# A gated cross-attention and local-attention block on one core: residual held transposed, rotary products on POOL, one ring of two PSUM banks, loops unrolled

## What is computed

```python
def attn_layer(x, Wqkv, qs, ksc, Wo):            # HEADS = 16, DIM_HEAD = 64, INNER = 1024
    q, k, v = jnp.split(x @ Wqkv, 3, -1)
    q = l2norm(q) * qs                           # per head
    k = l2norm(k) * ksc
    q = q * cos * scale + rotate_half(q) * sin * scale
    k = k * cos * inv + rotate_half(k) * sin * inv
    out = local_attention(q, k, v)               # windows of 32, each sees itself and the one before
    return out @ Wo
def ffn_layer(x, g, bln, W1, b1, W2, b2):        # inner width 341
    a, gate = jnp.split((layernorm(x) * g + bln) @ W1 + b1, 2, -1)
    return a * gelu(gate) @ W2 + b2
for i in range(6):
    x = attn_layer(shift_tokens(x), ...) + x     # shift_tokens: channels 64 to 127 come from the token before
    x = ffn_layer(shift_tokens(x), ...) + x
```

## Time and profile before

| | us |
|---|---|
| median of 3 runs | 2334.8 (2331.06 to 2336.24) |
| profiled execution, span from first to last instruction | 2340.2 |
| PE busy | 1958.2 |
| DVE busy | 1954.2 |
| ACT busy | 1449.0 |
| POOL busy | 1158.9 |

### The profile page before, as it was taken

How to read it: one execution, slowest core, us unless ns; L and a number is a source line. 1 busy time by engine, 2 the same in 40 slices (tenths; PEclk the granted TensorE clock), 3 DMA queues, 4 the chain that set the end, 5 groups by cost and what they waited for, 6 DMA issues and landing times.

```text
span 2340.2 us, 62168 instructions
## 1 busy us (share of the span) xinstructions
PE 1958.2 (84%) x19682; PEld 1270.3 (54%) x19682; DVE 1954.2 (84%) x3398; ACT 1449.0 (62%) x2645; POOL 1158.9 (50%) x868
## 2 busy tenths in 40 slices
PE   6678888888888888888888888888888888888886
PEld 4455555555555555555555555555555555555554
DVE  4689888888898898888888988888889889888784
ACT  2366666676666666666756666666666666666563
...
DMA packets 164546, 130.64 MB, mean 56 GB/s; under 512 B 42123, under 2 KB 157881, under 8 KB 164281
## 3 DMA queue, kind: packets, MB, share of 16 engines
...
...
## 4 chain that ended last, share of the span: by engine, by line
DVE 50%; issue 24%; PE 11%; ACT 9%; DVEq 3%; POOL 2%; ACTq 0%; DMA 0%; SPq 0%; POOLq 0%
DVE ra L1063 13%; DVE ss L1100 8%; DVE qkn L998 5%; DVE o L1096 5%; DVE rs L1069 4%; DVE mx L1004 4%; PE bank L716 3%; POOL rb L1188 2%; ACT qk L770 1%; ACT seed L788 1%; ACT L899 1%; DVE ssm L1103 1%; PE bank L527 1%; DVE step L987 1%; DVE step L984 1%
## 5 line engine op out<-in xcount | busy, mean ns | idle before, releaser
L1203 POOL TENSOR_TENSOR qkn<-qkn,rn 128x512 f32<-128x512 f32 x192 | 239.6, 1248 | 812.8 <-DVE rn L990 812.8
L1188 POOL TENSOR_TENSOR rb<-qk,tables 128x512 f32<-128x512 f32 x384 | 572.7, 1501 | 139.2 <-ACT qk L770 139.2
L527 PE MATMUL bank<-wqkv,xsT 128*128 (+1 forms) x1152 | 581.2, 614 | 12.6 <-ACT qk L770 10.3
L1063 DVE TENSOR_TENSOR ra<-qk,tables 128x512 f32<-128x512 f32 x384 | 467.1, 1255 | 92.1 <-issue 75.0
L1196 POOL TENSOR_TENSOR qkn<-ra,rb 128x512 f32<-128x512 f32 x192 | 268.6, 1399 | 122.6 <-DVE ra L1063 105.6
L770 ACT ACTIVATE qk<-bank 128x512 f32<-128x512 f32 x384 | 226.9, 591 | 158.2 <-PE bank L527 158.2
L527 PEld LDWEIGHTS bank<-wqkv,xsT 128*128 128x128 f32 x1152 | 192.9, 192 | 143.4 <-issue 118.7
L779 ACT ACTIVATE pr<-pr 128x512 f32<-128x512 f32 x192 | 120.9, 630 | 203.0 <-DVE pr L1007 198.6
L851 ACT ACTIVATE kB<-bank 64x512 f32<-64x512 f32 x384 | 226.4, 590 | 31.0 <-PE bank L583 26.3
L598 PE MATMUL bank<-vw,pT 128*32 128x128 f32 x6144 | 224.7, 291 | 11.3 <-ACT pT L796 8.9
L1100 DVE TENSOR_REDUCE ss<-sq 128x16 f32<-128x1024 f32 x192 | 231.0, 1203 | 0.5 <-ACT sq L857 0.5
...
## 6 DMA issues: line engine op xcount, KB each, us to landing
...
```

The source lines that it names most:

```text
L527: pe.matmul(QKV_BANKS[(3 * s + i) % 2][:, :], xsT[:, t * P:(t + 1) * P], wqkv[:, (g // B) % 2, cut], start=True, stop=True).then_inc(qkv_m ...
L1063: dve.tensor_tensor(heads(ra[:, cut]), heads(qk[:, s % 2, cut]), table.unsqueeze(1).to_broadcast([P, HU, DH]), ALU.mult).then_inc(cos_done, 1)
L1188: pool.tensor_tensor(halves(rb[:, cut]), halves(qk[:, s % 2, cut])[:, :, ::-1, :], table.rearrange("p (a d) -> p a d", a=2).unsqueeze(1).t ...
L1203: pool.tensor_tensor(k, k, spread(rn[:, HU:], DH), ALU.mult).then_inc(kn_done, 1)
```

## The change

1. **Loops unrolled.** A slot n stands for the old step; there are `SLOTS` = 192 + 14 slots. Every wait is on a constant.
2. **Residual transposed and shifted.** `xT` holds each sequence with channels on partitions, and channels 64 to 127 one column later. Columns 0 to 511 are then the shifted tokens. Shifts and their transposes go. The mean and variance of the layer norm come from PE, by a matrix of 1/128 (`mean`, `variance`), and `spread_rstd` spreads 1/std over the partitions.
3. **q and k normalised out of PSUM.** q and k of a unit lie in a bank pair `QK[u % 2]`; `squares` reads it, and DVE's `normalise_qk` writes both, scaled, to `qkn`. `copy_out` goes.
4. **Rotary products on POOL.** POOL multiplies `qkn` by cosine and sine, for q and k, into `turned`, and adds the two for k. For q PE transposes both products and adds them in PSUM.
5. **Wide projections.** `project_out` makes the output projection of a whole group in eight products of 512 columns (L458) in slot 5, and `down` three products of 512 columns (L528).
6. **A ring of two PSUM banks.** q, p, v, k and o of each slot, and all of the feed-forward part, take the two banks in turn. A turn waits until the turn before last has been read (`ring_read`).

The core of the diff:

```diff
-            def project(g, s, i):
-
-                n, t, half = 3 * (UPG * g + s) + i, s // HALVES, s % HALVES
-                pe.wait_ge(qkv_ev, past(n - 1))
-                cut = slice(i * INNER + half * UW, i * INNER + half * UW + UW)
-                pe.matmul(QKV_BANKS[(3 * s + i) % 2][:, :],
-                          xsT[:, t * P:(t + 1) * P], wqkv[:, (g // B) % 2, cut],
-                          start=True, stop=True).then_inc(qkv_mm, 1)
```

```diff
+                pe.wait_ge(kn_done, past(u - 1))
+                tok = xT[:, b, t * P:(t + 1) * P]
+                for i in range(2):
+                    cut = i * INNER + half * UW
+                    mm = pe.matmul(QK[u % 2][:, i * UW:(i + 1) * UW], tok, wqkv[:, layer % 2, cut:cut + UW],
+                                   start=True, stop=True)
+                mm.then_inc(qk_mm, 1)
...
+                for k in range(HP):
+                    blk = slice(k * P, (k + 1) * P)
+                    pe.matmul(RING[i % 2][:, blk], turned[:, u % 2, 0, blk], ident[:, :], is_transpose=True,
+                              start=True, stop=False)
+                    mm = pe.matmul(RING[i % 2][:, blk], turned[:, u % 2, 1, blk], ident[:, :], is_transpose=True,
+                                   start=False, stop=True)
+                mm.then_inc(ring_made[i % 2], 1)
...
+            def project_out(g):
+                if not 0 <= g < GROUPS:
+                    return
+                layer = g // B
+                i = turn("y", g)
+                pe.wait_ge(ring_read[i % 2], i // 2)
+                pe.wait_ge(*evicted("o", UPG * g + UPG - 1))
+                for k in range(KO):
+                    mm = pe.matmul(RING[i % 2][:, :], wo[:, layer % 2, k, :], oT[:, k, :],
+                                   start=(k == 0), stop=(k == KO - 1))
+                    if k == HP - 1:
+                        mm.then_inc(wo_half, 1)
+                mm.then_inc(ring_made[i % 2], 1)
+
...
+            for n in range(SLOTS):
+                g, s = n // UPG, n % UPG
+                queries_keys(n)
+                transpose_q(n - 2)
+                if s == 5:
+                    project_out(g - 1)
+                transpose_p(n - 4)
+                scores(n - 3)
+                values(n - 1)
+                transpose_k(n - 2)
+                attend(n - 4)
+                if s == 5:
+                    fold_bias(g - 1)
+                    mean(g - 1)
+                if s == 7:
+                    spread_rstd(g - 1)
+                transpose_o(n - 5)
+                if s == 6:
+                    variance(g - 1)
+                if s == 7:
+                    up("gate", 1, g - 1, 0)
+                    up("gate", 1, g - 1, 1)
+                    up("gate", 1, g - 1, 2)
+                    up("a", 0, g - 1, 0)
+                    up("a", 0, g - 1, 1)
+                if s == 0:
+                    up("a", 0, g - 2, 2)
+                if s == 1:
+                    down(g - 2)
+                if s == 2:
+                    transpose_out(g - 2)
```

```diff
-            def copy_out(g, s, i):
-
-                U = UPG * g + s
-                act.wait_ge(sq_done, past(U - 1))
-                act.wait_ge(cos_done, past(2 * (U - 1)))
-                act.wait_ge(sin_done, past(2 * (U - 1)))
-                act.wait_ge(qkv_mm, 3 * U + i + 1)
-                act.activation(qk[:, s % 2, i * UW:(i + 1) * UW], QKV_BANKS[(3 * s + i) % 2][:, :],
-                               ACT.Copy).then_inc(qkv_ev, 1)
...
-            def scale_q(g, s, U):
-
-                dve.wait_ge(rn_done, past(U))
-                dve.wait_ge(rotq_done, past(U))
-                q = heads(qkn[:, (s - 1) % 2, 0:UW])
-                dve.tensor_tensor(q, q, spread(rn[:, 0:HU], DH), ALU.mult).then_inc(qn_done, 1)
...
-                            dve.tensor_tensor(heads(ra[:, cut]), heads(qk[:, s % 2, cut]),
-                                              table.unsqueeze(1).to_broadcast([P, HU, DH]),
-                                              ALU.mult).then_inc(cos_done, 1)
```

```diff
+                dve.wait_ge(q_turned, past(2 * (u - 1)))
+                dve.wait_ge(rn_done, u + 1)
+                dve.tensor_tensor(heads(qkn[:, u % 2, 0:UW]), heads(QK[u % 2][:, 0:UW]), spread(r[:, 0:HU], DH),
+                                  ALU.mult).then_inc(qn_done, 1)
+                dve.wait_ge(k_turned, past(2 * (u - 1)))
+                dve.tensor_tensor(heads(qkn[:, u % 2, UW:]), heads(QK[u % 2][:, UW:]), spread(r[:, HU:], DH),
+                                  ALU.mult).then_inc(kn_done, 1)
```

```diff
+                norm_seed(n - 1)
+                copy_qT(n - 2)
+                copy_pT(n - 4)
```

The order in a slot of ACT after that is `copy_v(n - 1)`, `copy_kB(n - 2)`, `squares(n)`, `copy_oT(n - 5)`, `exponentials(n - 3)`; in slot 7 `gelu` of the group before stands ahead of the exponentials. DVE's and POOL's slots:

```diff
+            for n in range(SLOTS):
+                g, s = n // UPG, n % UPG
+                scale_o(n - 5)
+                if s == 6:
+                    centre(g - 1)
+                if s == 7:
+                    add_eps(g - 1)
+                if s == 1:
+                    gated(g - 2, 2)
+                sum_squares(n - 1)
+                if s == 2:
+                    add_ffn(g - 2)
+                if s == 7:
+                    rstd_newton(g - 1)
+                if s == 0:
+                    gated(g - 2, 0)
+                    gated(g - 2, 1)
+                sum_p(n - 4)
+                normalise_qk(n - 1)
+                if s == 5:
+                    add_attention(g - 1)
+                    add_bias(g - 1)
+                if s == 7:
+                    layer_norm(g - 1)
+                maxima(n - 3)
+                if s == 2:
+                    finish(g - 2)
+                invert_sum(n - 4)
+                less_maxima(n - 3)
```

```diff
+            def turn_by_cos(u, i):
+
+                g, layer, b, t, half = place(u)
+                table = tables[:, layer % 2, t, 2 * DH * i:2 * DH * i + DH]
+                return pool.tensor_tensor(heads(turned[:, u % 2, 2 * i, :]), heads(qkn[:, u % 2, i * UW:(i + 1) * UW]),
+                                          table.unsqueeze(1).to_broadcast([P, HU, DH]), ALU.mult)
...
+
+            def turn_q(u):
+                if not 0 <= u < UNITS:
+                    return
+                if u % UPG == 0:
+                    pool.wait_ge(table_ready, TPG + u // UPG)
+                if u >= 2:
+                    pool.wait_ge(*evicted("q", u - 2))
+                pool.wait_ge(qn_done, u + 1)
+                turn_by_cos(u, 0).then_inc(q_turned, 1)
+                turn_by_sin(u, 0).then_inc(q_turned, 1)
+
+            def turn_k(u):
+                if not 0 <= u < UNITS:
+                    return
+                if u >= 2:
+                    pool.wait_ge(*evicted("k", u - 2))
+                pool.wait_ge(kn_done, u + 1)
+                turn_by_cos(u, 1).then_inc(k_turned, 1)
+                turn_by_sin(u, 1).then_inc(k_turned, 1)
+
+            def sum_k(u):
+                if not 0 <= u < UNITS:
+                    return
+                pool.wait_ge(k_turned, 2 * u + 2)
+                k = turned[:, u % 2, 2, :]
+                pool.tensor_tensor(k, k, turned[:, u % 2, 3, :], ALU.add).then_inc(k_summed, 1)
...
+            for n in range(SLOTS):
+                g, s = n // UPG, n % UPG
+                sum_k(n - 2)
+                turn_q(n - 1)
+                turn_k(n - 1)
+                if s == 4:
+                    next_table(g)
```

1528 lines of the change are left out of this document (680 added, 848 removed).

## The result

The changed kernel takes 2149.0 us (median of four runs, 2138.2 to 2152.2) against 2335.5 us of the kernel before, run beside it: a ratio of 0.919 with a 95% interval of 0.917 to 0.922. The forecast was 2000 us with a range to 2130. The sign is right; of a gain forecast at 335 us, 186 came. The question for the experiments is where the other 149 us went.

What follows compares the result with a forecast made beforehand. PE was taken as the next bound: 75.9 + 1.5 = 77.4 us per group. Head 90.2, first group 64, 23 x 77.4 = 1780 and tail 54.4 make 1989 us; wakes make it 2000, range 1890 to 2130.

Steps and rivals of the forecast that it cites:

- the paragraph on SP: SP's ten v copies per unit take 6.3 us to issue, fit in PE's 7.2 us, and cost nothing.
- Theory A: From the follow-up: ACT's v eviction waits for SP's copies of unit u-2; a fifth vs buffer saves 3 to 5 us per group.
- the 1.5 for the lock: POOL's passes hold DVE's small operations; plain slots take 8.0 us, costing 1.5 us per group, 35 us in all.
- PE's own 75.9: PE's time per group of eight units: 57.7 us of unit work, 17.5 of feed-forward work, 0.7 of waiting.
- the pitch of 0.86: PE's start-to-start time for one 512-column product, 0.86 us, used for v, output, up, gate and down products.
- 12 for wakes: Wakes between engines, 0.06 us for each of 192 slots, raising the sum from 1989 to 2000 us.
- the holding of 16-column operations: DVE's 16-column operations wait for POOL's whole pass; times of up to 1.3 us would show it.
- rival 3: POOL and DVE lock each other in every slot: passes 1.48 us, slots 8.9, 2113 us in all; chance 0.20.
- The fourth rival: The ring makes PE sit through ACT's evictions: up to 2790 us, deciding at 1.75 us per unit; chance 0.06.
- the ring's own load: Five turns of matmuls, landing and evictions sum to 7.9 us on two banks, 4 us per slot; costed at nothing.
- Transposes with accumulation: q's added transposes on PE; two passes each would cost 0.9 us per unit, 170 us, and prove the forecast wrong.
- The chain of waits: The profile's chain that ended last; PE leading it in the changed kernel would show the forecast right.

Runs made afterwards that it cites:

- experiment 1: The changed kernel with five vs buffers in place of four, so a copy of v waits for the copies of unit u-3: 2018.6 us, ratio 0.864.
- 2: The changed kernel with two of SP's v copies per unit each issued as two halves, same bytes: 2293.9 us, ratio 0.982.
- 4: The changed kernel, four vs buffers, without the copies of the previous tile's last 32 tokens, eight issues per unit: 2040.4 us, ratio 0.873.
- experiment 6: DVE's clamp and refinement of 1/norm left out: 2137.5 us against the changed kernel's 2149.0; with five vs buffers 2017.4 against 2018.6.
- experiment 7: Against the five-vs-buffer kernel (2018.6 us): PE adds k's two products in place of POOL, 2100.5 us; or POOL adds q's in place of PE, 2136.1 us.

## Why the prediction missed

**The step that failed** is the paragraph on SP: "That fits in 7.2, and a copy has more than one slot before its product needs it. I cost it at nothing; without that cover it would be a floor of 6.3 us." Both halves are true (PE's L434 waited for no copy in the changed kernel) and neither was the question. I asked when the *reader* of the copies' target (PE's attention) needs them. I did not ask when the *writer* of their source needs the buffer back: ACT's v eviction, which sits in ACT's strict order and holds one of two ring banks. With that cover gone the cost was 130 us, shown by experiment 1, and from both sides by 2 and 4. It needed no new row: 6.3 us of issues, the wait in `copy_v` and the rule that SP starts behind attend were all there. The kernel before has the same wait ahead of its copy of v, and its list of waits has no entry for it: a slot was 10.0 us, longer than the 8.1 of this loop. Theory A's own 3 to 5 us per group were too low as well, for 5.7; the next part shows why. The other 19 of the 149 us stand under "PE's sum" below.

**Where the 130 us lie.** The view by line gives the idle time ahead of PE's instructions. Of the changed kernel (busy, mean of one | idle before, releaser):

```profile
L360 PE MATMUL qk_bank<-wqkv,xT 128*128 128x512 f32 x768 | 385.3, 627 | 21.1 <-issue 17.0 <-DVE qkn L823 2.9 <-ACT xT L609 1.3
...
L447 PE MATMUL ring_bank<-ident,o 128*128 128x128 f32 x768 | 124.8, 286 | 51.6 <-ACT vs L627 51.3
```

and of the one with five buffers:

```profile
L360 PE MATMUL qk_bank<-wqkv,xT 128*128 128x512 f32 x768 | 371.9, 608 | 22.7 <-issue 18.6 <-DVE qkn L823 2.8 <-ACT xT L609 1.3
...
L447 PE MATMUL ring_bank<-ident,o 128*128 128x128 f32 x768 | 124.3, 285 | 0.0
```

The busy line of the page of the kernel with five buffers:

```profile
PE 1938.9 (96%) x19010; PEld 1208.2 (60%) x19010; DVE 1432.6 (71%) x2757; ACT 1199.7 (59%) x2170; POOL 1237.5 (61%) x1012
```

The spans differ by 2148.5 - 2021.3 = 127.2 us. PE's time that is not busy is 2148.5 - 1983.9 = 164.6 us in the one and 82.4 in the other: 82 us of waiting, 51.6 of it at L447 and the rest at lines that follow (10.3 more at L528, 8.3 each at L371 and L496, 5.6 at L507). The other 45.0 us are *busy* time, for the same 19010 instructions: L360 takes 627 ns on average against 608. The granted clock explains some of it. One place of the changed kernel, PE's timeline and then the windows around it:

```profile
1122.98 1.88 PE L360 MATMUL qk_bank<-wqkv,xT 128*128 128x512 f32 x4
...
1131.40 0.66 PE L447 MATMUL ring_bank<-ident,o 128*128 128x128 f32 x4 [1.50 <-ACT vs L627]
1132.47 1.57 PE L496 MATMUL ring_bank<-mean_w,dsq 128*128 128x1 f32 x8 [0.42 <-ACT kB L654]
1133.90 3.76 PE L360 MATMUL qk_bank<-wqkv,xT 128*128 128x512 f32 x4
```

```profile
1118.00:1125.00 7.00, 7.00 (x84) 4.32 (x84) 5.26 (x10) 5.04 (x9) 2.39 (x2) 1.00 0.09 22
1125.00:1132.00 7.00, 5.50 (x86) 3.83 (x84) 4.35 (x10) 2.65 (x7) 5.00 (x5) 1.00 0.26 64
1132.50:1139.30 6.80, 6.80 (x21) 4.63 (x22) 4.17 (x12) 2.91 (x7) 1.95 (x2) 0.52 0.27 68
```

PE waits 1.50 us for the bank in the second window and 0.42 soon after; in the third the granted clock is 0.52, about 1.2 in place of 2.4 GHz, and the four projection products that take 1.88 us at 1122.98 take 3.76. Over the whole kernels the mean granted clock is 0.941 with the split copies, 0.965 in the changed kernel and 0.975 with five buffers. 0.035 of 2148.5 us is 75 us, 0.025 of 2021.3 is 51: some 25 of the 45 us. The other 20 us of busy time I can't place; matmul ends are modelled in the profile. So part of PE's waiting was paid again behind it. The Trainium skill, TensorE: Matmul & The Clock Gate, section "What's actually happening", says the same in kind, a gate that sets the share of clock pulses by how busy the engine has been; this case's rows give it its price, a fifth of the 127 us.

By slot, the starts of PE's attention products tell where in a group the time went. From one unit's to the next, in order from slot 4 to slot 4 of the next group, mean of the 22 whole groups with feed-forward work, the changed kernel takes 14.3, 8.6, 10.5, 15.4, 8.3, 12.1, 7.4 and 8.2 us, and the one with five buffers 14.2, 8.6, 8.3, 15.1, 8.3, 10.0, 7.4 and 7.35. So 2.2 us per group lie behind the attention of slot 6 (the place shown above is one of these), 2.1 behind that of slot 1, 0.8 in one of the plain slots, and five of the eight intervals are the same within 0.25. POOL's starts, with which I began, were a poor guide: for the three plain slots they read 8.5, 8.5 and 8.3 in the changed kernel and 8.5, 7.7 and 8.3 with five buffers, where PE takes 7.34.

**PE's sum.** With five buffers, where little but PE holds them, a plain slot took 7.34 us for 7.2, and a group without the once-in-a-layer work 77.5 for 77.4. That the groups agree is luck: the 1.5 for the lock was in the forecast and not in the run (experiment 6), so PE's own 75.9 was 1.6 us too low, 1.1 of it in the eight slots and the rest mostly at the gate products. The mis-sized term is the pitch of 0.86 for a 512-column product, which holds inside a train of them (the output projection adds the 6.9 us forecast for its eight) and not for a lone one. The lone product of v, in experiment 1's plain slot, goes from 1117.56 to 1118.52, 0.96 us, and the two sets of transposes behind it, k's to 1119.05, take 0.53 and 0.49 in place of 0.44; the two projections take 1.72 in place of 1.82. The five up and gate products, each for a bank of its own, take 4.86 us (1161.60 to 1166.46 in the same kernel) in place of 4.3, and the wait ahead of them 0.50 in place of 0.7.

Two terms were missing, put at nothing without a word. Folding the bias costs 1.36 us in each of six layers, 8 us. And at the first unit of each of the five later layers PE stands still. With five buffers, at the first such place (PE's projections, and SP's issue of the last quarter of the new layer's weights):

```profile
368.15 0.59 SPq L1135 DMA_DIRECT2D wqkv<-in_L_ffn_Wqkv_dram  x1
...
372.29 2.42 PE L360 MATMUL qk_bank<-wqkv,xT 128*128 128x512 f32 x4 [3.52 <-issue]
```

In the program this issue stands behind the unit's ten v copies, and PE's projections wait for it and for the part of `wo` issued at 368.78; by the page such DMAs land 3.5 and 3.3 us after their issue, here at 371.7 and 372.1. The view names no releaser, so this cause is read from the program and the times, and no run tested it. The five intervals take 19.1 to 20.7 us in place of 13.8, 29 us in all, the slower clock behind the wait among it (the four projection products took 2.42 us for 1.88). In the changed kernel the same five waits take 17.0 us, with five buffers 18.6, so they are no part of the 130.

Together, 23 x 1.6 = 37 us in the groups and 37 us in the two missing terms stand against 35 us for a lock that cost nothing, 12 for wakes and 5 in the first group (59.3 us for 64): 2022 us, where the profiled span is 2021.3. The bound itself is right (experiment 7), but that 2018.6 us is within 1% of the 2000 forecast for a kernel bound by PE is in part luck.

**DVE.** 66% busy (forecast under 75). The products of q and k from PSUM took what the earlier trace rows promised, in the view by line:

```profile
L820 DVE TENSOR_TENSOR qkn<-qk_bank,rn 128x512 f32<-128x512 f32 x192 | 132.9, 692 | 20.4 <-DVE rn L816 0.5
...
L804 DVE TENSOR_SCALAR ssm<-ss 128x16 f32<-128x16 f32 x192 | 79.8, 416 | 6.6
L811 DVE SCALAR_TENSOR_TENSOR step<-seed 128x16 f32<-128x16 f32 x192 | 59.4, 309 | 33.1 <-ACT seed L636 29.1
...
L814 DVE TENSOR_TENSOR step<-step,ssm 128x16 f32<-128x16 f32 x192 | 35.1, 183 | 6.6
```

q takes 0.69 us. The clamp at 0.42 and L811 at 0.31 us on average, against 0.18 for L814, show the holding of 16-column operations that the prediction asked for; it was there, but DVE had the time. In the slot above the clamp, started at 1188.03, ends as POOL's sum (1187.25, 1.28 us) does; L811 took 1.29 us once, started at 1196.34 with a POOL pass from 1196.33, and 0.17 at 1180.66, where POOL was idle. The Trainium skill, SBUF — State Buffer, section "SBUF: two separate sides", has operations with two SBUF inputs held, as L811, and those with fewer only in a two-port mode; no row shows which mode the clamp ran in, but it was held.

**POOL.** Passes of 1.27 us (forecast 1.27, rival 3 had 1.48), busy 58%. So the third rival was wrong in its mechanism, although its 2113 us lies nearest to the result. **The fourth rival**, PE sitting through evictions, came in part: 123 us are listed at L447 by PE and its weight loads, largely the same time, but from ACT's wait for a DMA and not from the length of evictions. PE's idle time at L447, 51.3 / 192 = 0.27 us per unit, is far from the 1.75 at which that rival decides. (The terms named for the ring's own load add up to 7.5 us per slot and not 7.9: 3.1 of matmuls, 0.8 of landing, 3.6 of evictions. It changes nothing.)

**Transposes with accumulation** took one pass each: L382 and L384 follow each other every 0.11 us, and experiment 7 prices four more at 0.43 us.

**The chain of waits** could not serve as the test I named: for the changed kernel it breaks off near the end and lists 1% for PE.
